# Moving the adds of zeros in a Flamingo block from the end of attention to the head of the experts

## The reference

```python
x = x + tanh(g_xattn[0]) * L0_xattn(layernorm(x), ctx_1024, ...)
x = x + tanh(g_ffn[0])   * L0_ffn(layernorm(x), router_w, up_w, down_w)
x = x + tanh(g_xattn[1]) * L1_xattn(layernorm(x), ctx_1024, ...)
x = x + tanh(g_ffn[1])   * L1_ffn(layernorm(x), gate_w, gate_b, w1, b1, w2, b2)

# L0_ffn: 8 experts, each token is sent to its 4 best (L1_ffn: to its 2 best)
h = gelu(einsum('bsd,edh->bseh', x, up_w))
expert_outputs = einsum('bseh,ehd->bsed', h, down_w)
output = sum(topk_weights[..., None] * gathered(expert_outputs, topk_indices), axis=2)
```

## Time and profile before

| | |
|---|---|
| median of 3 executions | 1607.34 us |
| lowest and highest | 1604.2 and 1611.0 us |
| the profiled execution | 1604.2 us, of which the span of the instructions 1602.3 us |
| mean granted clock of TensorE | 0.932 |
| DVE, ACT and POOL busy | 52%, 45% and 34% of the span |

### The profile page before, as it was taken

The page is one execution under the profiler, slowest core; times in us unless marked ns, Lnnn a source line. Parts: engine busy times, 40 slices in busy tenths (PEclk is TensorE's granted clock), DMA queues, the critical chain, the costliest instruction groups (busy, mean ns, idle before and its releaser), DMA issues. The chain is left out here.

```text
span 1602.3 us, 25436 instructions
## 1 busy us (share of the span) xinstructions
PE 1392.9 (87%) x9908; PEld 1288.8 (80%) x9908; DVE 834.8 (52%) x1654; ACT 713.1 (45%) x1375; POOL 552.5 (34%) x389
## 2 busy tenths in 40 slices
PE   5899989899867999999989995999889678987996
PEld 5776858768647899899889995988888668987996
DVE  3655656655664446446435223556666865455421
ACT  3354444444343454444444443454343425443553
POOL 1200001001025466566565441122120266566543
PEclk8899999999987999999999997998989769998998
DMA  3302031110115343443442223021202165444222
GB/s 128 120 24 67 27 95 43 52 61 27 66 51 156 94 86 81 116 106 92 105 104 47 47 42 100 24 88 41 72 30 80 54 193 119 102 106 109 48 42 35
DMA packets 72147, 123.30 MB, mean 77 GB/s; under 512 B 7440, under 2 KB 53152, under 8 KB 71968
## 3 DMA queue, kind: packets, MB, share of 16 engines
q1 hardware_dynamic: 46816, 81.92, 15.6%
q0 software_dynamic: 25152, 39.01, 13.4%
HBM read 96.12 MB, written 24.79 MB: 75 GB/s over the span
## 5 line engine op out<-in xcount | busy, mean ns | idle before, releaser
L2324 DVE TENSOR_TENSOR m_hidden_lo<-m_act_out,m_hidden_hi 128x512 fp32r<-128x512 f32 x224 | 162.6, 727 | 393.9 <-ACT m_hidden_hi L2267 368.5
L395 PE MATMUL banks<-m_down_hi,m_hidden_hi 128*128 128x256 f32 x896 | 267.9, 299 | 17.5 <-DVE m_hidden_lo L2324 11.3
L395 PE MATMUL banks<-m_down_hi,m_hidden_lo 128*128 128x256 f32 x896 | 263.7, 294 | 1.5 <-issue 1.5
L395 PE MATMUL banks<-m_down_lo,m_hidden_hi 128*128 128x256 f32 x896 | 263.9, 295 | 0.3 <-issue 0.3
L395 PEld LDWEIGHTS banks<-m_down_hi,m_hidden_hi 128*128 128x128 f32 x896 | 181.6, 203 | 22.2 <-issue 20.4
L395 PE MATMUL banks<-m_xt_hi,m_up_hi 128*128 128x256 f32 x640 | 186.6, 291 | 6.4 <-issue 6.4
L395 PE MATMUL banks<-m_xt_lo,m_up_hi 128*128 128x256 f32 x640 | 183.2, 286 | 0.0
L395 PE MATMUL banks<-m_xt_hi,m_up_lo 128*128 128x256 f32 x640 | 183.1, 286 | 0.0
L395 PEld LDWEIGHTS banks<-m_down_hi,m_hidden_lo 128*128 128x128 f32 x896 | 181.1, 202 | 1.7 <-issue 1.7
L395 PEld LDWEIGHTS banks<-m_down_lo,m_hidden_hi 128*128 128x128 f32 x896 | 181.5, 203 | 0.6 <-issue 0.6
L2401 POOL DMA_INDIRECT m_other_block<-rows,list_i x116 | 120.8, 1042 | 148.5 <-DVE list_i L1453 100.6
(11 more groups left out here) (367 smaller groups left out, 3555.0 us busy)
## 6 DMA issues: line engine op xcount, KB each, us to landing
stage<-in_down SPq DMA_DIRECT2D x22, 512.0 KB
stage<-in_ctx_cols SPq DMA_DIRECT2D x26, 402.0 KB
stage<-in_ctx_rows SPq DMA_DIRECT2D x20, 512.0 KB
stage<-in_up SPq DMA_DIRECT2D x20, 512.0 KB
m_stage<-in_up SPq DMA_DIRECT2D x11, 512.0 KB
m_stage<-in_down SPq DMA_DIRECT2D x10, 512.0 KB
rows<-xn SPq DMA_DIRECT2D x8, 528.0 KB, 3.7
stage<-in_ctx_picked SPq DMA_DIRECT2D x8, 512.0 KB
```

Of the source, the lines that this page charges most:

```text
L395: mm = q.e.matmul(dst, a, b, start=first and n == 0, stop=last and n == 2, skip_group_check=True)
L2324: q.e.tensor_tensor(lo, m.act[(n * HP + h) % ACTS], f32(hi), ALU.subtract).then_inc(*hidden_lo.mark((layer, n, h)))
```

## The change

The pair of adds moves from `gpsimd_early` to `gpsimd_experts`, behind the gathers of (0, 1) and (1, 0) and ahead of the reading of the counts. The waits that it had there (on the routing of an earlier batch, on the spare rows) go. The row numbers are written by VectorE behind `vector_finish_lists`, and `vector_keep_last` of block (0, 0) moves ahead of the conversions of the up weights and of block (0, 1). In layer 1 `m.y` gets another address; the fillers HOLD keep the others where they were.

```diff
-HOLD = (12884, 196)
+HOLD = (12372, 708)
@@ expert_memory, layer 1
                 m.xt_other = columns_other()
+                m.y = sb(n + "y", [P, BT, D], F32, st)[:, :, :]
...
                 m.xt_early = pair(n + "xt_early", [P, KD, BLOCK], st)
-                m.y = sb(n + "y", [P, BT, D], F32, st)[:, :, :]
@@ vector_early_list
-            q.wait_ge(*scored.of(layer, BATCH - 1, TT - 1))
-            q.e.tensor_scalar(exp[layer].i_last[1], col("spare"), BLOCK - 1.0, None, ALU.add).then_inc(*handed.mark(("last", layer, -2)))
@@ vector_experts
             q.wait_ge(*residual_out[layer].of(layer, b))
+            q.e.tensor_scalar(exp[layer].i_last[1], col("spare"), BLOCK - 1.0, None, ALU.add).then_inc(*handed.mark(("last", layer, -2)))
+            vector_keep_last(q, layer, 0, 0)
             convert(q, "d", [quarter(layer, 1, x) for x in range(KD)])
             vector_turn_block(q, layer, 0, 1)
-            vector_keep_last(q, layer, 0, 0)
@@ gpsimd_early
             gpsimd_gather(q, layer, 0, 0)
-            m = exp[layer]
-
-            q.wait_ge(*route_pe.of("choose", layer, BATCH - 2))
-            q.e.memset(m.y, 0.0).then_inc(*zeroed.mark(("y", layer)))
-            q.wait_ge(*zeroed.of("y", layer))
-            q.wait_ge(*handed.of("last", layer, -2))
-            q.wait_ge(*residual_out[layer].of("spare", layer))
-            for i in range(BT):
-                q.e.indirect_dma_start(out=acc_d[layer][0:BLOCK, :],
...
-            q.e.reg_add(adds_begun[0], adds_begun[0], 16 * BT)
@@ gpsimd_experts
             gpsimd_gather(q, layer, 0, 1)
             gpsimd_gather(q, layer, 1, 0)
+            q.e.memset(m.y, 0.0).then_inc(*zeroed.mark(("y", layer)))
+            q.wait_ge(*zeroed.of("y", layer))
+            q.wait_ge(*handed.of("last", layer, -2))
+            for i in range(BT):
+                q.e.indirect_dma_start(out=acc_d[layer], out_offset=bass.IndirectOffsetOnAxis(ap=m.i_last[1][:, i:i + 1], axis=0),
+                                       in_=m.y[:, i, :], in_offset=None, compute_op=ALU.add).then_inc(*adding.mark(None, 16))
+            q.e.reg_add(adds_begun[0], adds_begun[0], 16 * BT)
```

More of the change, by code:

```diff
@@ L2456, in gpsimd_early @@
             gpsimd_gather(q, layer, 0, 0)
-            m = exp[layer]
-            q.wait_ge(*route_pe.of("choose", layer, BATCH - 2))
-            q.e.memset(m.y, 0.0).then_inc(*zeroed.mark(("y", layer)))
-            q.wait_ge(*zeroed.of("y", layer))
-            q.wait_ge(*handed.of("last", layer, -2))
-            q.wait_ge(*residual_out[layer].of("spare", layer))
-            for i in range(BT):
-                q.e.indirect_dma_start(out=acc_d[layer][0:BLOCK, :],
-                                       out_offset=bass.IndirectOffsetOnAxis(ap=m.i_last[1][:, i:i + 1], axis=0),
-                                       in_=m.y[:, i, :], in_offset=None, compute_op=ALU.add).then_inc(*adding.mark(None, 16))
-            q.e.reg_add(adds_begun[0], adds_begun[0], 16 * BT)
         def gpsimd_experts(q, layer):
-            own = [other_there, added]
+            own, m = [other_there, added], exp[layer]
             q.wait_ge(*route_dve.of("listed", layer))
```

## The result

The changed kernel takes 1620.45 us (median of 19 runs, 1609.73 to 1624.82) beside 1607.02 us of the kernel before (19 runs, 1600.50 to 1614.99). The ratio is 1.0079, with a 95% interval of 1.0064 to 1.0094, so it is 12.7 us slower (10.3 to 15.1). The profiled execution took 1616.33 us, its span 1614.5.

What follows compares the result with a forecast made beforehand. TensorE sets the experts' pace; its ups of block (0, 1) waited 3.28 us for issue, reading counts. Terms 6.8 + 5.9 + 1.0 = 13.7 us gave 1617.9 from the profiled run, 1621.0 from the median; forecast 1620 us, range 1611 to 1628.

Steps and rivals of the forecast that it cites:

- Early adds cost nothing: End of attention, GpSimd: removing the adds gains nothing, as the queue then idles 9.34 and 11.70 us for VectorE's variance.
- y's address: Layer 1: y's new address changes neither shape nor bytes, priced at 0.
- The pair, 4.3 us: Expert head, GpSimd behind the gathers: memset 0.54, semaphore 0.28, two adds of 1.6 with 0.30 between, together 4.3 us.
- the 2.27 of the kernel before: GpSimd's longer add time beside VectorE's work; not used at the new place, where 1.6 us per add was taken.
- The landing, 2.6 us: GpSimd's wait behind the second add: zeros land 2.6 us after it, at 501.6, just after the counts' 501.25, so landing decides.
- The meeting of the subtractions, 4.64 us: VectorE's up-weight subtraction runs beside GpSimd's: 4.64 us from first cast to its end, with 2.56 as lower bound.
- The ups, +6.8 and +5.9: TensorE's up matmuls of block (0, 1) start 6.8 us later in layer 0 and 5.9 in layer 1.
- The clock, +1.0: TensorE's ups after the longer pause: a longer slow-clock stretch, 0.5 us taken for each layer.
- "Covered": the gather of (0, 2): Middle of TensorE's ups: block 2's gather lands by 510.5, before TensorE wants it near 511.3, so no cost.
- "Covered": ScalarE: ScalarE starts 7.7 us late; the hidden block's low part ends at 514.6, TensorE asks at 515.1, covered by half a microsecond.
- The sum of 13.7: Total forecast delay over both layers: 6.8 + 5.9 + 1.0 = 13.7 us.
- the decisive part: Expert head: VectorE's keeping copy waits for the adds' mark, idling from 488.8 to 501.7 with the conversions queued behind it.

Runs made afterwards that it cites:

- the seventh run: Kernel before, its early pair of adds at the end of attention issued again once landed: 1607.37 us, ratio 1.0004.
- the eighth: Changed kernel with y's old address and the filler HOLD in layer 1 put back: 1619.42 us, ratio 1.0077.
- sixth: Changed kernel with adds of 8 rows in place of 128: 1615.23 us, ratio 1.0071.
- the third: Kernel before with only VectorE's copies keeping the last weights and rows moved ahead of the conversions: 1605.24 us, ratio 1.0005.
- the first: Changed kernel with VectorE's keeping copies put back behind block (0, 1), so that only the adds move: 1615.15 us, ratio 1.0069.
- the fourth: Changed kernel with VectorE's keeping copies put back and GpSimd gathering (0, 2) ahead of the memset and adds: 1615.31 us, ratio 1.0047.
- second: Changed kernel with GpSimd gathering (0, 2) before its own subtraction of the up weights: 1614.23 us, ratio 1.0061.
- ninth: Kernel before with TensorE, ScalarE and VectorE reading the counts early, TensorE one behind each down: 1604.57 us, ratio 0.9982.
- the tenth: Kernel before with the counts read early and GpSimd gathering (0, 2) ahead of its subtraction of the up weights: 1599.43 us, ratio 0.9965.

## Why the prediction was right, and where not

- **Early adds cost nothing.** Shown by the seventh run, by the power at the same distance in the changed kernel, and by the stretch behind the early gather.
- **y's address.** Shown: the eighth.
- **The pair, 4.3 us.** 0.54, then 498.74 to 502.26: 4.33 us from the start of the memset. Right, and mostly a fixed price (sixth). The adds took 1.63 and 1.58 us, so that it was right to leave the 2.27 of the kernel before out.
- **The landing, 2.6 us.** 2.24 (504.5 - 502.26); in layer 1 the mark came at 1316.5, 2.15 us behind the pair. That is 0.4 too dear. It did decide, as forecast, but not by much: the counts on GpSimd's queue were read at 503.8, 0.7 us earlier. The rest of the difference in the start of the copy comes from the gathers, which end 5.75 us behind the copy of the counts, 0.74 earlier than before (494.63 - 488.14 = 6.49): VectorE idled beside them, and the first two took 1.01 and 0.95 us for 1.25 and 1.47. The other runs confirm it in layer 0: the gathers end at 5.8 us in the third, where VectorE idles too, and at 6.6 in the first and the fourth, where it converts. I had carried their end over unchanged.
- **The meeting of the subtractions, 4.64 us.** 504.68 to 506.01 + 3.24: 4.57. *The Trainium skill's page "SBUF — State Buffer", section "SBUF: two separate sides", has VectorE and GpSimd share ports;* the row agrees, 3.24 us beside GpSimd's subtraction and 1.23 without it (second).
- **The ups, +6.8 and +5.9.** They came +5.4 and +4.5 later, each 1.4 too dear in the forecast: 0.7 the gathers, 0.4 the landing, the rest in small steps.
- **The clock, +1.0.** Not seen. From the first up to the first down it took 8.44 us in the changed kernel less the 0.69 of the wait, 7.75; before, 7.78. In layer 1, less the waits, 9.38 and 9.23. The clock in windows of 2 us:

```profile
508.00:510.00 2.00, 0.03 (x1) 0.03 (x1) 2.00 (x4) 0.00 (x0) 1.85 (x2) 0.50 0.34 84
510.00:512.00 2.00, 2.00 (x9) 2.00 (x10) 1.97 (x3) 0.07 (x1) 1.67 (x3) 0.50 1.01 281
512.00:514.00 2.00, 2.00 (x16) 2.00 (x15) 2.00 (x1) 1.98 (x3) 1.91 (x1) 0.79 0.71 282
```

  It was at the lower level (1.2 GHz) when the ups began and left it some 3 us later, as in the earlier trace rows (the full clock ahead of the pause, of which the prediction speaks, is in the trace, 1.00 from 494.14 to 496.14, but not in those rows). A pause of 9.6 us cost no more slow matmuls than one of 3.3. The stretch itself scatters: 8.44 us in the eighth kernel, without any wait for (0, 2), and 8.78 in the seventh behind a pause of only 3.38, so that 0.5 us a layer is less than one profile can tell.
- **"Covered": the gather of (0, 2).** This step failed. The prediction let the gather land at 510.5 ahead of TensorE's 511.3, with 2.5 us for its two parts and the 2.6 of an add for its landing. TensorE waited 0.69 us in layer 0 and 0.63 in layer 1. In layer 0, the mark, and from issue to landing of the two parts:

```profile
L2408 POOLq EVENT_SEMAPHORE  x1: 17/17/17, 515.0 to 515.0; - x1
...
DMA to landing us min/median/max: 4.5/4.9/5.3
```

  The two parts took 3.18 us (508.32 to 511.50), beside VectorE's work. The second landed 4.5 us behind its start, at 515.0, which is 3.5 behind its end, and GpSimd's queue marked it at once. Both terms were too small, by 0.7 and 0.9 us.
- **"Covered": ScalarE.** Right, and as narrow as forecast. Its first y came 6.7 us late against the copy of the counts (19.76 for 13.11; 7.7 in the forecast), VectorE's low part of the hidden block ended at 517.88, and TensorE asked for it at 518.42 without waiting. In the second run, where the ups start earlier, it is not covered.
- **Layer 1 behind the ups.** The turn of (1, 0) came after 4.37 us of idling, 2.45 before, both ended by TensorE's own queue. These 1.9 us are in the measured 7.2, and I have no cause for them: the same gap was 2.2 and 2.7 us in the seventh and third kernel, and 1.4 to 3.8 in the others.

So the mechanism was the forecast one, and that the numbers meet so well (1620 us beside 1620.45) is partly luck. The sum of 13.7 is near the 13.2 of the two heads because errors offset each other: 2.8 us too much in the ups and 1.0 in the clock, against 1.3 of missed waits for (0, 2) and 1.9 in layer 1. And "the decisive part" was too narrow. VectorE's wait is what ends last in the changed kernel, but it is one of three that hang on one mark: GpSimd, whose loop over the blocks begins with the wait for the pair, marks it late, and VectorE's copies, ScalarE's first y, and GpSimd's own conversion, gather and mark of (0, 2) all stand behind it. Taking one away leaves 10 to 13 us at the heads and 8 to 11 in the time (first, second, fourth). To take all three away, the zeros would have to come from another buffer than y and be counted apart from the adds; that was not tried, so that nothing else of the pair costs is not shown.

## What to carry to other kernels

When a wait is moved to a busy place, list everything behind it on every engine, the marks on the waiting queue too, and price the latest of them; removing the wait that the profile names may only bring the next. A wait that falls in the middle of TensorE's work can cost more than its length, by the clock. Work in a wait that something else ends is free, here twice over even. A pair of small indirect adds took some 6.5 us at this head with its memset and its landing, and still 5.4 to 5.8 with 8 rows in place of 128, since the reading of the counts was then last or nearly so. Register loads that end an idle time as "issue" were a real bound here, worth moving to where the engine has work in hand, but only while nothing later covers them.

## What was not expected of the hardware

- A copy of 128x2 elements, else 0.16 us, took 2.20 us on VectorE (498.14, ninth) beside a subtraction of GpSimd, and 2.51 in the tenth, again for as long as GpSimd's ran:

```profile
502.69 2.51 DVE L2321 COPY m_w_last<-m_w_first 128x2 f32<-128x2 f32 x1
```

```profile
502.76 2.40 POOL L497 TENSOR_TENSOR m_up_lo<-m_stage,m_up_hi 128x1024 fp32r<-128x1024 f32 x1
```

  Which of VectorE's instructions pays depends on which stands there when GpSimd starts.
- An indirect add is almost all fixed price for GpSimd: 1.36 us for 8 rows, 1.58 for 128. Its landing is not: 1.5 us for 2.15 in layer 1.
